# Attention query operand written by block-diagonal loads instead of VectorE copies, and half of one PSUM evacuation moved from ScalarE to VectorE

## What is computed

```python
x = x + 0.5 * ffn(layernorm(x), weight, bias)          # 512x512, both operands rounded to an FP6 grid in blocks of 32
x = x + attention(layernorm(x), qkv_w, qkv_b, rpb, proj_w, proj_b)
x = x + 0.5 * ffn(layernorm(x), weight, bias)

# attention: 16 heads of 32 channels, each token sees 13 neighbours
qkv = (x @ qkv_w.T + qkv_b);  q, k, v = qkv[0] * 32 ** -0.5, qkv[1], qkv[2]
attn = softmax(einsum('bhld,bhlkd->bhlk', q, k[:, :, nbr, :]) + rpb[:, bidx])
out = einsum('bhlk,bhlkd->bhld', attn, v[:, :, nbr, :]) @ proj_w.T + proj_b
```

## Time and profile before

| | |
|---|---|
| median of 3 runs (lowest, highest) | 3540.44 us (3539.46, 3541.88) |
| span of the profiled execution | 3541.7 us |
| its own time | not listed apart; the run nearest to its span is 3541.88 us |
| attention phase in it, first to last score matmul | 1751.4 to 2990.4 us |
| busy in its whole span: TensorE, VectorE, ScalarE, GpSimd | 2897.5, 2759.5, 2021.9, 1993.0 us |
| DMA packets, bytes, mean rate | 274586, 449.41 MB, 127 GB/s |

### The profile page before, as it was taken

How to read it: one execution, slowest core, us unless ns; L and a number is a source line. 1 busy time by engine, 2 the same in 40 slices (tenths; PEclk the granted TensorE clock), 3 DMA queues, 4 the chain that set the end, 5 groups by cost and what they waited for, 6 DMA issues and landing times. The chain is left out here.

```text
span 3541.7 us, 67789 instructions
## 1 busy us (share of the span) xinstructions
PE 2897.5 (82%) x24864; PEld 1690.4 (48%) x24864; DVE 2759.5 (78%) x3553; ACT 2021.9 (57%) x2451; POOL 1993.0 (56%) x1497
## 2 busy tenths in 40 slices
PE   0399999999999999999677777777777777399999
PEld 0244444444444444444356555555555555244444
DVE  7366666666666666666599999999999998599995
ACT  3355556555556555564566666666666657466553
POOL 3454455544555445543166665666666666588883
PEclk9699999999999999999889988999999889699999
DMA  2123332333323332332465554555555553234432
GB/s 72 60 84 119 108 108 95 108 111 115 102 101 107 107 119 93 103 114 84 146 175 163 170 170 148 166 161 179 152 162 162 169 160 98 107 143 155 153 142 83
DMA packets 274586, 449.41 MB, mean 127 GB/s; under 512 B 15368, under 2 KB 181280, under 8 KB 266144
## 3 DMA queue, kind: packets, MB, share of 16 engines
q1 hardware_dynamic: 274336, 445.54, 39.4%
HBM read 243.85 MB, written 201.38 MB: 126 GB/s over the span
## 5 line engine op out<-in xcount | busy, mean ns | idle before, releaser
L761 DVE TENSOR_TENSOR fq_out_lo<-fq_val,fq_out_hi 128x512 f16<-128x512 f32 x384 | 460.6, 1237 | 289.8 <-ACT fq_out_hi L825 289.8
L1125 DVE COPY att_q_bd<-att_q_in 32x1024 f16<-32x1024 f16 x512 | 624.0, 1219 | 5.9 <-DMA att_q_in<-q_parts 0.7
L942 PE MATMUL fq_acc<-fq_y_hi_t,w_qkv 128*128 128x512 f16 x2048 | 614.3, 379 | 1.6 <-ACT fq_y_hi_t L838 1.6
L825 ACT CAST fq_out_hi<-fq_val 128x512 f16<-128x512 f32 x384 | 237.2, 618 | 318.9 <-DVE fq_val L758 310.8
L1250 PE MATMUL att_s_ps<-att_k,att_q_bd 128*128 128x44 f16 x6144 | 192.0, 187 | 271.2 <-DVE att_q_bd L1125 251.0
L942 PE MATMUL fq_acc<-fq_y_lo_t,w_qkv 128*128 128x512 f16 x1024 | 388.1, 379 | 0.0
L1228 POOL TENSOR_TENSOR att_score<-att_score,att_rtotal 128x704 f32<-128x704 f32 x128 | 211.2, 1650 | 226.3 <-DVE att_rtotal L1116 226.3
L1210 POOL TENSOR_TENSOR att_score<-att_score,att_top 128x704 f32<-128x704 f32 x128 | 188.3, 1471 | 245.1 <-DVE att_top L1105 245.1
L1165 ACT ACTIVATE att_ctx<-att_o_ps 32x512 f32<-32x512 f32 x512 | 300.6, 587 | 44.8 <-PE att_o_ps L1275 38.6
L1285 PE MATMUL att_y_ps<-w_proj,att_ctx_t_hi 128*128 128x512 f16 x1024 | 320.3, 396 | 2.4 <-DVE att_x L1150 2.2
L1250 PEld LDWEIGHTS att_s_ps<-att_k,att_q_bd 128*128 128x128 f16 x6144 | 178.8, 100 | 290.9 <-issue 238.3
(11 more groups left out here) (189 smaller groups left out, 6707.1 us busy)
## 6 DMA issues: line engine op xcount, KB each, us to landing
att_v<-v_parts SPq DMA_DIRECT2D x96, 704.0 KB
att_k<-k_parts SPq DMA_DIRECT2D x64, 524.0 KB, 7.4
fq_x<-in_L_attn_x SPq DMA_DIRECT2D x32, 1024.0 KB, 6.9
x_after_ffn<-fq_x SPq DMA_DIRECT2D x32, 1024.0 KB, 4.3
att_q_in<-q_parts SPq DMA_DIRECT2D x32, 1024.0 KB, 7.2
att_x<-x_after_ffn SPq DMA_DIRECT2D x32, 1024.0 KB, 5.6
x_after_attention<-att_x SPq DMA_DIRECT2D x32, 1024.0 KB, 4.3
ffn_x_ring<-x_after_attention SPq DMA_DIRECT2D x32, 1024.0 KB, 6.2
```

Source lines behind the costliest of these rows:

```text
L761: dve.tensor_tensor(out=out[1][:, b], in0=val[:, b % RING], in1=out[0][:, b], op=ALU.subtract).then_inc(s["out_lo"], 1)
L825: act.copy(out[0][:, b], val[:, b % RING]).then_inc(s["out_hi"], 1)
L942: op = pe.matmul(acc[:, b % RING], w, m, start=(kc == 0 and (a, c) == (0, 0)), stop=(kc == KC - 1 and (a, c) == PARTS[-1]))
L1125: op = dve.tensor_copy(q_bd[rows, u.u % 2, :, :, :, h, :].rearrange("p a g c q -> p (a g) c q"), q_in[rows, g.u, :, :, place * P:(place + ...
```

## The change

Each DMA now writes one head's rows for one half of a group, one part (high or low) and one channel block straight into the diagonal blocks, in runs of 32 float16 numbers (64 bytes). There are 4 heads x 2 parts x 4 blocks = 32 DMAs for a half and 64 for a group, each of 32 partitions x 8 chunks. `q_in`, `spread` and its semaphore go. `q_bd` holds one buffer for each half of a group (2 units). The SyncE order changes, `out_second` moves to VectorE, and the order of stages inside a turn changes on VectorE and GpSimd.

```diff
-        q_in = sb("q_in", [P, 2, 2, KC, GROUP], F16)
-        q_bd = sb("q_bd", [P, 2, 2, KC, CHUNKS, HG, CHUNK], F16)
+        q_bd = sb("q_bd", [P, 2, 2, KC, QCHUNKS, P], F16)
```

SyncE:

```diff
-                def queries_and_keys(g):
-                    need(sp, s["spread"], (g.n - 1) * UG)
-                    sp.dma_start(q_in[:, g.u].rearrange("p a g n -> p a (g n)"),
-                                 scratch["q"][:, :, bass.ds(g.n * KC * GROUP, KC * GROUP)].rearrange("a p n -> p a n")
-                                 ).then_inc(q_loaded[g.u], 16)
...
+                def queries(g, half):
+                    need(sp, s["scored"], (2 * g.n + half - 1) * QUNITS * PAIRS)
+                    if isinstance(g.h, int) and g.n == 0:
+                        sp.wait_ge(s["q_zero"], half + 1)
+                    for h in range(HG):
+                        rows = slice(h * HEAD_DIM, (h + 1) * HEAD_DIM)
+                        columns = scratch["q"][:, rows, bass.ds(g.n * KC * GROUP, KC * GROUP)].rearrange(
+                            "a p (g n) -> p a g n", g=KC)[:, :, :, half * QCOLS:(half + 1) * QCOLS]
+                        for part in range(2):
+                            for kc in range(KC):
+                                sp.dma_start(q_bd[rows, half, part, kc, :, rows],
+                                             columns[:, part, kc].rearrange("p (c q) -> p c q", q=CHUNK)).then_inc(
+                                                 q_loaded[half], 16)
...
+                def body(t):
+                    keys_in(t)
+                    values(t.back(1))
+                    queries(t, 0)
+                    residual_out(t.back(3))
+                    queries(t, 1)
+                    residual_in(t.back(1))
```

VectorE:

```diff
-                dve.memset(q_bd[:], 0.0).then_inc(s["q_zero"], 1)
-                dve.wait_ge(s["q_zero"], 1)
+                for i in range(2):
+                    dve.memset(q_bd[:, i], 0.0).then_inc(s["q_zero"], 1)
...
-                def spread(u):
...
-                    for h in range(HG):
-                        rows = slice(h * HEAD_DIM, (h + 1) * HEAD_DIM)
-                        op = dve.tensor_copy(q_bd[rows, u.u % 2, :, :, :, h, :].rearrange("p a g c q -> p (a g) c q"),
-                                             q_in[rows, g.u, :, :, place * P:(place + 1) * P].rearrange(
-                                                 "p a g (c q) -> p (a g) c q", q=CHUNK))
-                    op.then_inc(s["spread"], 1)
+                def second_half(u):
+                    need(dve, s["turned"], PAIRS * u.n + 2)
+                    need(dve, s["weighted"], u.n - 1)
+                    dve.tensor_copy(prob_t[:, u.u % 2, HALF:], t_ps[:]).then_inc(s["out_second"], 1)
```

ScalarE:

```diff
-                    if w.within(UNITS):
-                        need(act, s["turned"], PAIRS * w.n + 2)
-                        act.copy(prob_t[:, w.u % 2, HALF:], t_ps[:]).then_inc(s["out_second"], 1)
```

TensorE:

```diff
-                    need(pe, s["spread"], u.n + 1)
+                    half = place // QUNITS
+                    if place % QUNITS == 0:
+                        pe.wait_ge(q_loaded[half], 16 * HG * 2 * KC * (g.n + 1))
...
-                                    q = q_bd[:, u.u % 2, a, kc, c].rearrange("p h q -> p (h q)")
+                                    q = q_bd[:, half, a, kc, place % QUNITS * CHUNKS + c, :]
```

More of the change, by code:

```diff
@@ L998, in attention_phase @@
     ROWS = PAIRS * KC * 2
+    QUNITS = UG // 2
+    QCHUNKS = QUNITS * CHUNKS
+    QCOLS = QUNITS * P
     HALF = ROWS // PAIRS
@@ L1032, in attention_phase @@
         stored = [sem(f"stored{i}") for i in range(2)]
-        names = ("q_zero", "v_zero", "p_zero", "spread", "scored", "biased", "topped", "lowered", "exped", "totalled",
+        names = ("q_zero", "v_zero", "p_zero", "scored", "biased", "topped", "lowered", "exped", "totalled",
                  "inverted", "normed", "p_hi", "p_lo", "turned", "out_first", "out_second", "weighted", "context",
@@ L1047, in _, with keys_in @@
             def _(sp):
[L1048 removed]
+                def queries(g, half):
                     if not g.within(GROUPS):
                         return
[L1051 to L1054 removed]
+                    need(sp, s["scored"], (2 * g.n + half - 1) * QUNITS * PAIRS)
[10 more added lines that the diff above has]
+                                                 q_loaded[half], 16)
+                def keys_in(g):
+                    if not g.within(GROUPS):
+                        return
                     need(sp, s["scored"], (g.n - 1) * UG * PAIRS)
@@ L1059, in queries_and_keys @@
                             k_loaded[g.u], 16)
-                def body(t):
[L1062 to L1078, removed]
@@ new lines, in values @@
+                def values(g):
+                    if not g.within(GROUPS):
+                        return
+                    need(sp, s["weighted"], (g.n - 1) * UG)
+                    sp.wait_ge(s["v_zero"], 2)
+                    for part, at in ((0, 0), (0, WIN), (1, 0)):
+                        rows = scratch["v"][part, bass.ds(g.n * GROUP, GROUP + 2 * NS), :]
+                        windows = bass.AP(rows.tensor, rows.offset, [[C, WIN], [CHUNK * C, GROUP // CHUNK], [1, C]])
+                        sp.dma_start(vals[at:at + WIN, g.u, :, part, :], windows).then_inc(v_loaded[g.u], 16)
@@ new lines, in residual_out, with residual_in @@
+                def residual_out(g):
+                    if not g.within(GROUPS):
+                        return
+                    need(sp, s["summed"], (g.n + 1) * UG)
+                    sp.dma_start(dst_v[:, bass.ds(g.n * UG, UG), :], x[:, g.u]).then_inc(stored[g.u], 16)
+                def residual_in(g):
+                    if not g.within(GROUPS):
+                        return
+                    need(sp, stored[g.u], 16 * g.h)
+                    sp.dma_start(x[:, g.u], src_v[:, bass.ds(g.n * UG, UG), :]).then_inc(x_loaded[g.u], 16)
@@ L1133, in body @@
                         bias(u)
-                    if t.within(UNITS):
-                        spread(t)
                     u = t.back(LAG_N)
@@ L1138, in body @@
                         totals(u)
[L1139 to L1144, removed]
                     u = t.back(LAG_OUT)
@@ L1152, in body @@
                                                  op1=ALU.add).then_inc(s["summed"], 1)
+                    u = t.back(LAG_T)
+                    if u.within(UNITS):
+                        second_half(u)
+                    u = t.back(LAG_C)
+                    if u.within(UNITS):
+                        need(dve, s["ctx_hi"], u.n + 1)
+                        need(dve, s["projected"], u.n - 1)
+                        dve.tensor_tensor(out=ctx_t[1][:, u.u % 2], in0=ctx_f[:, u.u % 2], in1=ctx_t[0][:, u.u % 2],
+                                          op=ALU.subtract).then_inc(s["ctx_lo"], 1)
                 run(dve, body)
@@ L1206, in body @@
                 def body(t):
+                    u = t.back(LAG_P)
+                    if u.within(UNITS):
+                        need(pool, s["p_hi"], u.n + 1)
+                        pool.tensor_tensor(out=prob[:, u.u % 2, :, WIN:2 * WIN], in0=score[:, u.u % 4],
+                                           in1=prob[:, u.u % 2, :, 0:WIN], op=ALU.subtract).then_inc(s["p_lo"], 1)
                     u = t.back(LAG_S)
@@ L1212, in body @@
                                            op=ALU.subtract).then_inc(s["lowered"], 1)
+                    u = t.back(LAG_N)
+                    if u.within(UNITS):
+                        need(pool, s["inverted"], u.n + 1)
+                        pool.tensor_tensor(out=score[:, u.u % 4], in0=score[:, u.u % 4],
+                                           in1=rtotal[:, u.u % 2].unsqueeze(2).to_broadcast(wide),
+                                           op=ALU.mult).then_inc(s["normed"], 1)
                     u = t.back(LAG_C)
@@ L1219, in body @@
                                            op=ALU.add).then_inc(s["x_biased"], 1)
[L1220 to L1230, removed]
                 run(pool, body)
```

7 lines of the change are left out of this document (2 added, 5 removed).

## The result

The changed kernel takes 4057.98 us (median of 4 runs, 4054.01 to 4060.58) against 3539.95 us for the kernel before (4 runs, 3537.19 to 3541.88). The ratio is 1.1461, 95% interval 1.1445 to 1.1478: 518 us slower. The forecast was 3960 us with a range of 3690 to 4420.

The account below looks back on a forecast made before the run. SyncE's query DMA issue, standing still behind V, was to set the pace: 20.3 + 14.0 + 0.5 + 18.2 + 0.3 = 53.3 us a loop group. Last scores then come 420 us later: 3540 + 420 = 3960 us, range 3690 to 4420.

Parts of the forecast that it names:

- What bound it before: Attention phase: VectorE, 94% busy, set the pace by its block-diagonal copies, 4.88 us of its 9.35 us a unit.
- the order cost nothing: Attention turns: new stage order free while another engine sets the pace, VectorE having over 2 us a unit free.
- The issue: SyncE, attention loop: 64 query DMAs a group, 0.57 us each, 36.5 us, between 26 and 51; 0.44 each outside the loop.
- rival (a): SyncE's query DMAs: issue costs 0.80 us each, 66.3 us a loop group, 4370 us in all; chance 0.28.
- The queueing: SyncE stands still behind residual, K and V, 20.3 us a group, getting only 7.5 query DMAs ahead; 14.0 us for 24.5 more.
- The packets: Query transfer: 17 packets per DMA and engine at 14 ns, 0.24 us, hidden below 0.57 us between issues.
- rival (b): Query transfer: packets cost 50 ns, pace 0.85 us a DMA, group 69 us, 4500 us in all; chance 0.07.
- (c): SyncE: query issues overlap V's drain, no standing still, 41.4 us a group, +50, 3590 us; chance 0.07.
- (d): SyncE: cheap addresses, 0.41 us an issue, with standing still; 44.1 us a group, +163, 3700 us; chance 0.06.
- (e): SyncE: issue overlaps the drain at 0.41 us or less (threshold below 0.31 with standing still); -240, 3300 us; chance 0.06.
- the serial reading: Query DMAs run one after another at the skill's fixed cost each: about 130 us a group, some 6000 us in all.
- 0.3 of loop arithmetic: SyncE, attention loop: the loop's own register work adds 0.3 us a group.

Follow-up runs that it names:

- experiment 2: Kernel before, with only the evacuation of prob_t's second half moved from ScalarE to VectorE; 3604.13 us, ratio 1.017.
- experiment 1: Changed kernel with the evacuation of prob_t's second half given back to ScalarE; 4066.14 us, ratio to before 1.147.
- 9: Changed kernel with q stored half by half in DRAM, 16 query DMAs a group in place of 64, same 64-byte packets; 3464.07 us, ratio 0.9778.
- 12: Changed kernel with merged query DMAs and V issued by ScalarE, but two of four heads spread by VectorE copies again; 3419.58 us, ratio 0.9648.
- 3: Changed kernel with the three V loads spread among the query DMAs, same DMAs and counts; 3869.72 us, ratio 1.0931.
- 6: Changed kernel with each V load cut to 44 packets in place of 704; 3728.66 us, ratio 1.0541.
- 8: Changed kernel with the three V loads issued by ScalarE instead of SyncE; 3857.99 us, ratio 1.0889.
- experiment 4: Changed kernel with 4 of 8 chunks left out of each query DMA, as many DMAs, half the 64-byte packets; 3970.26 us, ratio 1.1205.
- experiment 5: Changed kernel with the low part of q never loaded, 32 query DMAs a group in place of 64; 3493.96 us, ratio 0.9877.
- 7: Changed kernel with V loads cut to 44 packets and 4 of 8 chunks left out of each query DMA; 3693.37 us, ratio 1.0441.

## Why the prediction was right, and what it missed

**What bound it before** was right. VectorE's copies were 4.88 us a unit and are gone; the new copy took 0.68 us against 0.65 taken (experiment 2), and it costs nothing here (experiment 1). But VectorE has 5.8 us of work a unit now (696.87 us in 120.8 units), not 5.1. Two of its other instructions got longer: the low part of the context from 654 to 884 ns on average, and the scaling of the total, an instruction on 16 numbers a partition, before and after (duration ns min/median/max):

```profile
L1113 DVE TENSOR_SCALAR att_total<-att_total x128: 174/174/1003, 1764.8 to 2999.7; 128x16 f32<-128x16 f32 x128
L1139 DVE TENSOR_SCALAR att_total<-att_total x128: 174/650/1258, 1768.8 to 3514.3; 128x16 f32<-128x16 f32 x128
```

In experiment 2, with the old order of stages, the low part of the context stays at 653 ns; in experiments 1, 9 and 12, with the new order, it takes 922, 1043 and 897. That fits the new order as the cause; no run changed the order alone. The prediction had the order cost nothing "while another engine sets the pace", and so it was; but VectorE's slack is smaller than it said. ScalarE's 5.3 and TensorE's 7.4 us a unit came out at 5.3 and 7.6.

**The issue**: the prediction took 0.57 us from one query DMA to the next in the loop, one address computation each. The computations are there, 1792 of them; the DMA instruction took 317 ns and not K's 373, so the step was 0.50. The 601 ns of the 32-partition rows, rival (a), did not come; what makes those twelve DMAs dearer stays open. In the first group it was 31.41 us for 64, 0.49 against 0.44 taken.

**The queueing** was called the step that decides, and experiments 3, 6 and 8 bear it out. Summed from the start of the residual's load at 2432.48, the first part with K, V and 32 queries ends at 2466.6: 34.1 us, against 20.3 + 14.0 = 34.3 forecast. On average over the loop, this part takes 34.3 where it holds no jump back. That the sum agrees so well is in part luck: the issue is some 2 us cheaper than forecast, and the standing still as much dearer. The second 32 took 18.6 to 19.0 against 18.2, and again two errors cancel: 0.50 each in place of 0.57, and 2.8 of standing still behind the residual store, which the prediction had at none.

**The packets** stayed below the issue, as forecast; rival (b), with 69 us a group, fell with the pace of 55.9, and experiment 4 bears that out. **Rivals (c), (d) and (e)**: (c) needed no standing still behind V, (d) an issue of 0.41 us, (e) both; none was so. Two side sums of the prediction are off, without effect on the forecast: the threshold in (e) with standing still comes to 0.33 us and not 0.31, and the serial reading of 130 us a group to some 6400 us and not 6000.

**The term that was mis-sized** is "0.3 of loop arithmetic". The loop's jump back costs SyncE 5.4 to 6.0 us each time, once in two groups, against 0.3 in the same place without a jump: 2.6 us a group. The queues that load instruction code, in the changed kernel (packets, MB, share of 16 engines):

```profile
q8 instruction: 223, 3.65, 0.4%
q14 instruction: 96, 0.79, 0.1%
```

Before, the second had 27 packets and the first the same 223. SyncE's code got longer (128 query DMAs with their register work in one loop turn). The window of one pause, 2486.4 to 2491.9, holds one packet of the second queue:

```profile
q14 instruction: 1, 0.01, 0.4%
```

So it is in all 13 pauses of this trace: a packet of 8 KB on this queue starts 3.6 to 4.1 us after the last DMA instruction, and the next DMA instruction starts 1.8 to 1.9 us behind it. The seven kernels with 64 query DMAs have 91 such pauses together, all with the packet 1.8 to 2.0 us before their end. SyncE goes on when that code has come; no run lengthened or shortened the loop's code alone, with the DMAs left as they are. The pause is gone with 32 or fewer query DMAs a group. In experiment 5 the same place in the stream is a gap of 0.66 us, from 2475.39 to 2476.05:

```profile
2475.00 0.39 SPq L1096 DMA_DIRECT2D att_x<-x_after_ffn  x1
2476.05 0.95 SPq L1073 DMA_DIRECT2D att_k<-k_parts  x2
```

28 groups x (55.9 - 53.3) = 73 us, and the first four groups ended at 1929.6 instead of 1908, 22 us: together 95 of the 98 us between forecast and result. Of the 22, 4 x 64 x 0.05 = 13 are the dearer issue outside the loop; the rest is more standing still.

**The experiments' own misses** have one thing in common: I treated issue and transfer as if either hid the other fully. Where SyncE was expected to run at 0.50 us a DMA, it went at 0.6 to 0.7, so 3, 6, 7 and 8 came out 40 to 180 us above the ends of their ranges. In 7 over half of the missing time goes with the code packets; how the rest divides between these and the shared DMA engines stays open.

## What to carry to other kernels

Count the DMAs that a change adds to one issuing engine, at the distance from one to the next in its own stream (here 0.50 us with an address computation each), and add the transfers that stand ahead of them in that queue: an engine that appears in no table of busy time can be the bound. Look also at the length of its loop body. Merge the DMAs before judging the idea: here the same 64-byte runs in 16 DMAs a group were 2.2% faster than the kernel before, in 64 they were 14.6% slower. When a copy moves from an engine to the DMA engines, moving half of it can beat both ends (3419.58 us, against 3449.08 with all of it moved and 3545.51 with none).

## What was not expected of the hardware

A long loop body on SyncE cost 5.4 to 6.0 us at each jump back, with 69 more code packets in the trace, one of them 1.8 to 1.9 us before the end of each pause. A query DMA of 32 partitions from DRAM took 317 ns of issue, less than K's 373 with 128 partitions, while twelve of 32 partitions at the kernel's start, from SBUF to SBUF, take 601. A single issue took 1.64 us beside one 16 KB code packet that held one DMA engine for 1.3 us, and 106 of 119 such packets lie beside a long issue. A VectorE instruction on 16 numbers a partition went from 174 to 650 ns at the median in the changed kernel.
